# Gate scores on 32-column strips of the PE array, and one transpose to turn a group's scores back

## The chip, the cores and the metric

The kernel runs on one core of one Trainium2 chip, as one launch. The metric is the device time of that launch in microseconds (us). Three timed runs of the kernel before gave 1331.63, 1332.4 and 1335.52 us; the median is 1332.4 us.

## The reference, cut to what matters

Four blocks are applied in turn to 3125 rows of 256 features, each on the layer-normalised rows and added to the rows: a graph convolution of two layers (GNN 0), a mixture of 8 experts (FFN 0), a second graph convolution (GNN 1), a shared MLP with 4 small experts (FFN 1). The second layer of each graph convolution and the gate scores of the block that follows it are what the change is about:

```python
def _sage_conv(x, src, dst, Wl, bl, Wr):          # one layer
    agg = segment_sum(x[src], dst)                # sum over the neighbours
    mean = agg / max(cnt, 1)
    return mean @ Wl.T + bl + x @ Wr.T

x = x + _L0_gnn_ref(_layernorm(x), ...)           # two such layers
# FFN 0: x normalised, all in f32
gate_scores = x @ Wg + bg                         # 256 features to E = 8 scores a row
_, idx = top_k(gate_scores, 2)                    # the two best experts of each row
...
x = x + _L1_gnn_ref(_layernorm(x), ...)
# FFN 1
gates = softmax(x @ gW + gb)                      # 256 features to E = 4 scores a row
topv, topi = top_k(gates, 2)
```

## The kernel before, in words

The 3125 rows are padded to 25 tiles of 128. `adj` holds the matrix of edge counts in SBUF as f16, and a sum over neighbours is a product of `adj` with the rows, of which `l_parts` holds a high and a low f16 half. The function `second_conv` does the second layer of a graph convolution and, on the same rows, the norm and the gate scores of the block that follows. It is called twice: once with names that begin with `l_` (8 scores, `routing=True`, followed by the experts of FFN 0 in the same program block) and once with names that begin with `l1b_` (4 scores, followed by FFN 1). They are called the first and the second pass here.

In each pass TensorE (PE) first works through 25 steps of `dense` (f32, L2025) and `early` (tiles 0 to 9, L2049). Then it does one tile of rows after another, tiles 10 to 24 (`one_tile`): 50 matmuls of 128x256 f16 each (L2064). The rest is done for 7 groups of tiles of 4, 4, 4, 4, 4, 3 and 2 tiles (`SIZES`), and PE's part of it is put between the matmuls of `one_tile` by the table `BETWEEN`: the entry `(13, 1): [("rank", 0), ("score", 1)]` says that rank of group 0 and score of group 1 stand behind tile 13, and `(22, 0)` would be in the middle of tile 22. Per group:

- `turn(c)`: 2 transposes a tile, so that the features lie on the partitions (L2075, `l_dense`).
- ScalarE (ACT) takes them to SBUF, into `own` (L1975).
- `score(c)`: two matmuls, one for each half of the 256 features, with the gate's weights `wg` as the stationary operand (128 rows, 8 or 4 columns) and all the group's rows as the moving one (up to 512 columns), f32, into 8 or 4 partitions of the bank `extra` (L2084). The trace shows each f32 matmul as two passes with a weight load each.
- ACT copies that to `flat`, 8 or 4 partitions by up to 512 (L1986, `take_flat`).
- `back(c)`: one transpose a tile, of 8x128, to 128x8 in `l_sum` (L2095). For group 0 it waits until VectorE (DVE) has added the first ten tiles' sums, since it writes to the bank of the last two of them.
- DVE adds the bias. In the first pass it picks the two best experts (`choose`), PE sums the masks (`rank`, L2103 and L2104), DVE works out the places (`put`), and GpSimd (POOL) scatters the rows (L1757).

The order on each engine is the order in which the code issues; nothing reorders it. On the last tile, `BETWEEN[(24, 1)]` runs the rest of groups 5 and 6 one after another. In the second pass PE does products of FFN 1 there (`head`, L1488).

Before the groups, DVE sets up small things behind `take(24)`: L1907 to L1915.

Of the kernel before, what the change touches and what calls it, by code (L numbers as in the profile page):

```python
# [18 lines left out]
P = 128  # L19
D = 256  # L20
KD = D // P
# [1517 lines left out]
MOST = max(SIZES)  # L1539
assert STARTS[-1] == TILES  # L1540
# [35 lines left out]
def second_conv(nc, io, g, adj, parts, tag, names, gate, rows_from, rows_to, work, sums_left, routing=False, final=None):  # L1576
# [4 lines left out]
    with ExitStack() as ctx:  # L1581
# [26 lines left out]
        if routing:  # L1608
# [15 lines left out]
        wg = pr.sb("gate_w", [P, KD, E], F32)  # L1624
        bg = pr.sb("gate_b", [P, E], F32)
# [6 lines left out]
        flat = room[0:E, KD * MOST * P:(KD + 1) * MOST * P]  # L1632
# [4 lines left out]
        score_at, ranks_at, totals_at = (last_bank[:, at:at + MOST * E].rearrange("p (t e) -> p t e", e=E) for at in (0, 64, 128))  # L1637
# [4 lines left out]
            "ranked", "placed", "place_ready", "head_mm", "head_took", "init", "chain", "route_chain", "hi_in", "hi_used")  # L1642
# [141 lines left out]
        def _(dve):  # L1784
# [125 lines left out]
            dve.wait_ge(s["gate_in"], 32)  # L1910
            if routing:
                dve.wait_ge(s["consts"], 4)
                nc.vector.tensor_copy(row_id[:, :], row_i[:, :]).then_inc(s["init"], 1)
                nc.vector.memset(pre[:, MOST, :], 0.0).then_inc(s["init"], 1)
                nc.vector.tensor_copy(down[:, :], down_i[:, :]).then_inc(s["init"], 1)  # L1915
                dve.wait_ge(s["init"], 4)
                finish_early()
                for c in range(FINISHES):
                    choose(c)
                    put(c)  # L1920
                    if c + 2 < FINISHES:
                        finish(c + 2)
                nc.vector.tensor_copy(g["counts"][:, :], pre[:, SIZES[-1], :]).then_inc(s["init"], 1)
                dve.wait_ge(s["init"], 5)
                table.vector(dve)
                follow["vector"](dve)
            else:
                dve.wait_ge(s["init"], 1)
                finish_early()
                final.constants(nc, ch)  # L1930
                for c in range(FINISHES):
                    take_scores(c)
                    if c + 2 < FINISHES:
                        finish(c + 2)

        @block.scalar
        def _(act):
# [44 lines left out]
            def take_flat(c):  # L1982
                act.wait_ge(s["multiplied"], c + 1)
                if c >= 1:
                    act.wait_ge(s["scored"], c)
                nc.scalar.activation(flat[:, 0:SIZES[c] * P], extra[0:E, 0:SIZES[c] * P], ACT.Copy).then_inc(s["flat_ready"], 1)  # L1986
# [30 lines left out]
        def _(pe):  # L2017
# [61 lines left out]
            def score(c):  # L2079
                pe.wait_ge(s["xt_ready"], KD * (c + 1))  # L2080
                if c >= 1:
                    pe.wait_ge(s["flat_ready"], c)
                for f in range(KD):
                    ins = nc.tensor.matmul(extra[0:E, 0:SIZES[c] * P], wg[:, f, :], own[:, f, 0:SIZES[c] * P],  # L2084
                                           start=f == 0, stop=f == KD - 1)
                ins.then_inc(s["multiplied"], 1)

            def back(c):
# [5 lines left out]
                for t in range(SIZES[c]):  # L2094
                    ins = nc.tensor.transpose(score_at[:, t, :], flat[:, t * P:(t + 1) * P], g["ident"][0:E, 0:E])  # L2095
                ins.then_inc(s["scored"], 1)

            def rank(c):
# [4 lines left out]
                nc.tensor.matmul(last_bank[:, 64:64 + SIZES[c] * E], tri[:, :], mask[:, 0:SIZES[c], :], start=True, stop=True)  # L2103
                nc.tensor.matmul(last_bank[:, 128:128 + SIZES[c] * E], all1[:, :], mask[:, 0:SIZES[c], :], start=True, stop=True  # L2104
# [27 lines left out]
            pe.wait_ge(s["gate_in"], 32)  # L2132
# [799 lines left out]
```

## Time and profile before

| what | value |
|---|---|
| timed runs, median | 1332.4 us |
| profiled execution, span from first to last instruction | 1304.2 us |
| median less span, outside what the trace shows | 28.2 us |
| PE busy | 1220.4 us, 94% |
| DVE busy | 588.7 us, 45% |
| ACT busy | 360.1 us, 28% |
| POOL busy | 159.5 us, 12% |
| mean granted clock of PE | 0.980 |

PE is busy nearly all the time. Its matmuls are pipelined: a matmul's time in the trace is that from its start to its result, 273 ns for a 128x256 f16 one, while the next one starts long before that. What a group of matmuls costs PE is therefore read from the starts: from its first to the first of what follows. The first pass's tiles 10 to 24 lie at about 404 to 504 us of the span, the second's at about 1050 to 1154 us.

### The profile page before, as it was taken

What the parts mean: (1) busy time and instruction counts of PE and PEld (TensorE: products, weight loads), DVE (VectorE), ACT (ScalarE), POOL (GpSimd) and SP (SyncE); (2) the same over time, 40 slices, a digit from 0 to 9 for tenths busy, and PEclk for the clock granted to TensorE, in tenths of its full rate; (3) what the DMA queues carried; (4) which work ended last, traced back from release to release, by engine and by line L of the source; (5) the groups of instructions that cost most, each with busy time, mean ns of one, the idle gap of its engine ahead of it and who ended that gap; (6) DMA issues with size and microseconds to landing.
All of it is one profiled execution on the core that took longest, in us unless ns stands there. A gap on an engine that the chain in (4) does not pass through costs nothing. (4 is left out here: it accounts for less than half of the span.)

```text
span 1304.2 us, 22005 instructions
## 1 busy us (share of the span) xinstructions
PE 1220.4 (94%) x7906; PEld 913.8 (70%) x7906; DVE 588.7 (45%) x1563; ACT 360.1 (28%) x765; POOL 159.5 (12%) x151
## 2 busy tenths in 40 slices
PE   5969999998999997999999779999989999999998
PEld 3648888885667785787888657555556677866675
DVE  7968888853445657211111165000034363246544
ACT  3544444432221101333333234200022201124333
POOL 4100000000000336433443300000000000000000
PEclk9989999999999998999999979999999999999999
DMA  6400000014652235445655331120056434126001
GB/s 198 159 24 10 18 9 18 18 36 143 174 147 95 88 105 179 93 92 111 137 105 102 52 125 61 57 65 29 15 152 178 130 117 146 50 72 203 20 20 38
DMA packets 133085, 117.08 MB, mean 90 GB/s; under 512 B 22706, under 2 KB 121395, under 8 KB 133008
## 3 DMA queue, kind: packets, MB, share of 16 engines
q1 hardware_dynamic: 101760, 76.03, 20.1%
q0 software_dynamic: 11984, 18.77, 7.4%
q10 hardware_dynamic: 19264, 21.24, 4.8%
q8 instruction: 50, 0.82, 0.3%
q14 instruction: 27, 0.22, 0.1%
HBM read 67.01 MB, written 48.99 MB: 89 GB/s over the span
## 5 line engine op out<-in xcount | busy, mean ns | idle before, releaser
L1276 PE MATMUL b_pa<-adj,l_parts 128*128 (+1 forms) x1100 | 148.5, 287 | 2.5 <-ACT ring L1212 2.5
L1276 PEld LDWEIGHTS b_pa<-adj,l_parts 128*128 128x128 f16 x1100 | 104.9, 98 | 28.1 <-issue 4.4
L1218 ACT ACTIVATE adj<-b_pw 128x450 f32 (+1 forms) x176 | 86.8, 546 | 107.8 <-PE b_pw L1263 102.0
L561 DVE TENSOR_TENSOR ring<-it,key 128x1800 f16<-128x1800 f16 x88 | 96.4, 1096 | 36.3 <-PE b_pw L1263 36.0
L2400 PE MATMUL l_sum<-l_parts,ring 128*128 128x256 f32 x448 | 104.1, 385 | 5.2 <-ACT ring L2470 2.3
L2535 POOL DMA_INDIRECT x<-ring,l_ids_now x56 | 87.3, 1559 | 131.6 <-DVE ring L2500 103.2
L2400 PEld LDWEIGHTS l_sum<-l_parts,ring 128*128 128x128 f32 x448 | 82.9, 190 | 22.4 <-ACT ring L2470 12.3
L1263 PE MATMUL b_pw<-ring,room 128*128 128x150 f16 x1056 | 87.3, 233 | 9.9 <-DVE room L561 8.1
L2500 DVE TENSOR_TENSOR ring<-l_sum,l_parts 128x256 f32 (+1 forms) x56 | 23.6, 425 | 153.2 <-PE l_sum L2400 153.2
L1263 PEld LDWEIGHTS b_pw<-ring,room 128*128 128x128 f16 x1056 | 77.7, 100 | 15.2 <-DVE room L561 9.6
L2064 PE MATMUL l1b_sum<-l_parts,adj 128*128 128x256 f16 x750 | 86.5, 276 | 0.0
L2064 PE MATMUL l_sum<-l_parts,adj 128*128 128x256 f16 x750 | 84.9, 273 | 0.0
L561 DVE TENSOR_TENSOR room<-ib,low 128x1536 f16<-128x1536 f16 x88 | 83.8, 952 | 0.0
L2064 PEld LDWEIGHTS l1b_sum<-l_parts,adj 128*128 128x128 f16 x750 | 73.3, 99 | 13.5 <-issue 4.3
L2064 PEld LDWEIGHTS l_sum<-l_parts,adj 128*128 128x128 f16 x750 | 72.3, 98 | 12.9 <-issue 4.5
L1795 DVE SCALAR_TENSOR_TENSOR l_parts<-l1b_dense,scale,l_parts 128x256 f16<-128x256 f32 x25 | 12.1, 484 | 141.0 <-ACT l_parts L1950 141.0
L2755 ACT ACTIVATE l_parts<-m_bank,adj 128x320 f32<-128x320 f32 x82 | 42.7, 527 | 73.3 <-PE m_bank L2693 44.7
L2049 PEld LDWEIGHTS l_sum<-l_parts,adj 128*128 128x128 f16 x500 | 48.8, 98 | 19.9 <-issue 12.9
L2049 PEld LDWEIGHTS l1b_sum<-l_parts,adj 128*128 128x128 f16 x500 | 48.8, 98 | 19.4 <-issue 13.1
L501 PE MATMUL n_agg<-adj,l_parts 128*128 128x448 f16 (+1 forms) x300 | 60.6, 361 | 0.0
L2049 PE MATMUL l_sum<-l_parts,adj 128*128 128x256 f16 x500 | 58.5, 273 | 0.8 <-DVE l_parts L1795 0.8
L2049 PE MATMUL l1b_sum<-l_parts,adj 128*128 128x256 f16 x500 | 58.5, 273 | 0.4 <-DVE l_parts L1795 0.4
(384 smaller groups left out, 1741.4 us busy)
## 6 DMA issues: line engine op xcount, KB each, us to landing
ring<-sums_and_zt SPq DMA_DIRECT2D x50, 256.0 KB, 3.1
l_parts<-in_L_ffn_W SPq DMA_DIRECT2D x16, 512.0 KB, 5.0
l_parts<-slots_in SPq DMA_DIRECT2D x28, 257.0 KB, 2.7
pre<-room ACTq DMA_DIRECT2D x34, 128.0 KB, 1.8
ring<-inv SPq DMA_DIRECT2D x50, 64.0 KB, 3.7
sums_and_zt<-room ACTq DMA_DIRECT2D x5, 640.0 KB, 3.4
adj<-xt SPq DMA_DIRECT2D x5, 640.0 KB, 4.4
adj<-x SPq DMA_DIRECT2D x5, 640.0 KB, 5.7
```

Of the source, the lines that this page charges most:

```text
L501: ins = nc.tensor.matmul(pairs[n % 3][f][:, 0:size], parts[:, k, a, f * P:(f + 1) * P], moving, start=start and a == 0, stop=stop and a == 1)
L561: return nc.vector.tensor_tensor(out.rearrange("p r (h two) -> p r h two", two=2), names[:, 0:width].rearrange("p (h two) -> p h two", two ...
L1218: ins = nc.scalar.activation(adj[:, :, ds(group * GW * W + b * BANKW * W, BANKW * W)].rearrange("p k (w j) -> p w k j", j=W), pw[u % SLOT ...
L1263: ins = nc.tensor.matmul(to, low[:, n, :], sel[:, n, :], start=i == 0, stop=i == VIS - 1)
L1276: ins = nc.tensor.matmul(pa[f][:, :], parts[:, k, a, f * P:(f + 1) * P], adj[:, k, ds(r * BW, BW)], start=k == 0 and a == 0, stop=k == TIL ...
L1795: nc.vector.scalar_tensor_tensor(parts[:, k, 1, :], dense_bank[k % 2][:, 0:D], scale, parts[:, k, 0, :], ALU.mult, ALU.subtract).then_inc( ...
L2049: ins = nc.tensor.matmul(acc(t), adj[:, k, t * P:(t + 1) * P], parts[:, k, a, :], start=k == 0 and a == 0 and opens(t), stop=k == TILES - ...
L2064: ins = nc.tensor.matmul(acc(t), adj[:, k, t * P:(t + 1) * P], parts[:, k, a, :], start=k == 0 and a == 0 and opens(t), stop=k == TILES - ...
L2400: ins = nc.tensor.matmul(to[t], h[:, n, t * P:(t + 1) * P], w2[:, u, n, :], start=n == 0, stop=n == HB - 1)
L2500: nc.vector.tensor_tensor(y[:, half, t, :].rearrange("p a d -> p (a d)"), products[t], b2[:, u, :], ALU.add).then_inc(s["y_done"], 1)
L2535: pool.indirect_dma_start(out=g["x1"], in_=y[:, half, t, :], in_offset=None, compute_op=ALU.add, out_offset=bass.IndirectOffsetOnAxis(ap=i ...
L2755: nc.scalar.activation(to, b[:, 0:SUB], ACT.Relu, bias=bias).then_inc(s["act_took"], 1)
```

## The change

The gate's weights are copied once, by DVE, into `strips_of_wg`: 32 columns for each half of the features, of which the first 8 or 4 are the gate's and the rest are zero. `score` multiplies each row tile of 128 rows on its own: tile t of the group writes to partitions 32t to 32t+31 of `extra`, that is, through columns 32t to 32t+31 of the array. So it has 8 matmuls of 32x128 where it had 2 of 8x512. ACT copies 128 partitions by 128 (`flat`), and `back` is one transpose of 128x128. The scores then stand 32 columns apart in the bank, and the places of ranks and totals in it move to columns 128 and 192.

```diff
+STRIP = 32
+RANKS_AT, TOTALS_AT = MOST * STRIP, MOST * STRIP + 64
...
+        strips_of_wg = held[1][:, 0:KD * STRIP].rearrange("p (k e) -> p k e", k=KD)
...
-        flat = room[0:E, KD * MOST * P:(KD + 1) * MOST * P]
+        flat = room[:, KD * MOST * P:KD * MOST * P + P]
...
+            dve.wait_ge(s["pre_out1"], 16 * uses(1))
+            nc.vector.memset(strips_of_wg[:, :, E:STRIP], 0.0)
+            nc.vector.tensor_copy(strips_of_wg[:, :, 0:E], wg[:, :, :]).then_inc(s["gate_padded"], 1)
...
-                nc.scalar.activation(flat[:, 0:SIZES[c] * P], extra[0:E, 0:SIZES[c] * P], ACT.Copy).then_inc(s["flat_ready"], 1)
+                strips = SIZES[c] * STRIP
+                nc.scalar.activation(flat[0:strips, :], extra[0:strips, 0:P], ACT.Copy).then_inc(s["flat_ready"], 1)
...
+                if c == 0:
+                    pe.wait_ge(s["gate_padded"], 1)
...
                 for f in range(KD):
-                    ins = nc.tensor.matmul(extra[0:E, 0:SIZES[c] * P], wg[:, f, :], own[:, f, 0:SIZES[c] * P],
-                                           start=f == 0, stop=f == KD - 1)
+                    for t in range(SIZES[c]):
+                        ins = nc.tensor.matmul(extra[t * STRIP:(t + 1) * STRIP, 0:P], strips_of_wg[:, f, :], own[:, f, t * P:(t + 1) * P],
+                                               start=f == 0, stop=f == KD - 1)
...
-                for t in range(SIZES[c]):
-                    ins = nc.tensor.transpose(score_at[:, t, :], flat[:, t * P:(t + 1) * P], g["ident"][0:E, 0:E])
-                ins.then_inc(s["scored"], 1)
+                nc.tensor.transpose(last_bank[:, 0:P], flat[:, :], g["ident"][:, :]).then_inc(s["scored"], 1)
```

PE in the first pass, tile 12, from `score` of group 0 to behind its `back`, before (the sums are L2064, score L2084, back L2095):

```order
L2064 MATMUL l_sum<-l_parts,adj 128x256 x22
L2084 MATMUL l_extra<-room,l_gate_w 8x512 x2
L2064 MATMUL l_sum<-l_parts,adj 128x256 x26
L2095 MATMUL l_sum<-ident,room 128x8 x4
L2064 MATMUL l_sum<-l_parts,adj 128x256 x2
```

The same place of the changed kernel (the sums are L2073, score L2096, back L2106):

```order
L2073 MATMUL l_sum<-l_parts,adj 128x256 x22
L2096 MATMUL l_extra<-room 32x128 x8
L2073 MATMUL l_sum<-l_parts,adj 128x256 x26
L2106 MATMUL l_sum<-ident,room 128x128
L2073 MATMUL l_sum<-l_parts,adj 128x256 x2
```

Nothing is placed elsewhere among the sums; two matmuls became eight, and four transposes one.

DVE in the first pass, between the last step of `dense` and the sums of group 0, before (`l_tmp` is scratch of the norm; L1804 adds the bias to group 0's rows, L1810 its sums):

```order
L1907 TENSOR_SCALAR l_by_row<-l_by_row,unscale 128x25
L1908 MEMSET l_tmp 128x30
L1913 CAST l_row_id<-l_row_i 128x25
L1914 MEMSET l_pre 128x8
L1915 CAST l_down<-l_down_i 128x8
L1804 TENSOR_TENSOR l_rows<-l_rows,l_bias 128x4x256
L1810 SCALAR_TENSOR_TENSOR l_rows<-l_sum,l_by_row,l_rows 128x256 x4
```

The same place of the changed kernel:

```order
L1912 TENSOR_SCALAR l_by_row<-l_by_row,unscale 128x25
L1913 MEMSET l_tmp 128x30
L1917 MEMSET room 128x2x24
L1918 COPY room<-l_gate_w 128x2x8
L1921 CAST l_row_id<-l_row_i 128x25
L1922 MEMSET l_pre 128x8
L1923 CAST l_down<-l_down_i 128x8
L1809 TENSOR_TENSOR l_rows<-l_rows,l_bias 128x4x256
L1815 SCALAR_TENSOR_TENSOR l_rows<-l_sum,l_by_row,l_rows 128x256 x4
```

A memset and a copy now stand ahead of the sums of group 0.

## Rows read from the trace of the kernel before

**Rows 1.** Stretches of both passes; busy us (instructions) by engine, granted clock, DMA
```profile
425.00:500.00 75.00, 75.00 (x641) 61.48 (x641) 47.22 (x214) 7.51 (x16) 30.41 (x32) 1.00 0.30 101
1080.00:1150.00 70.00, 70.00 (x590) 56.22 (x588) 23.04 (x82) 6.21 (x14) 0.00 (x0) 1.00 0.30 97
```

**Rows 2.** Timeline of weight loads: start us, us, engine, line, what, [idle before]
```profile
1081.25 0.09 PEld L2084 LDWEIGHTS l1b_extra<-room,l1b_gate_w 128*4 128x4 f32 x2 [0.21 <-issue]
1081.68 0.09 PEld L2084 LDWEIGHTS l1b_extra<-room,l1b_gate_w 128*4 128x4 f32 x1 [0.34 <-issue]
1082.11 0.09 PEld L2084 LDWEIGHTS l1b_extra<-room,l1b_gate_w 128*4 128x4 f32 x1 [0.34 <-issue]
1083.06 0.22 PEld L2064 LDWEIGHTS l1b_sum<-l_parts,adj 128*128 128x128 f16 x3 [0.86 <-issue]
```

**Rows 3.** Timeline of PE, second pass, a turn and the sums behind it
```profile
1077.44 1.04 PE L2075 MATMUL l1b_dense<-ident,ring 128*128 128x128 f32 x8
1078.32 3.00 PE L2064 MATMUL l1b_sum<-l_parts,adj 128*128 128x256 f16 x26
```

**Rows 4.** Timeline of PE around back of group 1, second pass
```profile
1085.80 2.89 PE L2064 MATMUL l1b_sum<-l_parts,adj 128*128 128x256 f16 x25
1088.62 0.41 PE L2095 MATMUL l1b_sum<-ident,room 4*128 4x4 f32 x4
1088.96 2.25 PE L2064 MATMUL l1b_sum<-l_parts,adj 128*128 128x256 f16 x19
```

**Rows 5.** Timeline of PE, the two short matmuls of rank
```profile
431.39 0.18 PE L2103 MATMUL l_sum<-l_mask,l_tri 128*128 128x32 f16 x1
431.42 0.18 PE L2104 MATMUL l_sum<-l_mask,l_all 128*128 128x32 f16 x1
```

**Rows 6.** Line L2084, weight loads: ns min/median/max, first and last start us, forms
```profile
L2084 PEld LDWEIGHTS l_extra<-room,l_gate_w x28: 85/90/137, 418.6 to 512.0; 128*8 128x8 f32 x28
```

**Rows 7.** Timeline of PE, back of group 0 in either pass
```profile
424.74 0.38 PE L2095 MATMUL l_sum<-ident,room 8*128 8x8 f32 x4 [1.27 <-DVE ring L1810]
...
1072.84 0.38 PE L2095 MATMUL l1b_sum<-ident,room 4*128 4x4 f32 x4 [3.08 <-DVE ring L1810]
```

**Rows 8.** Timeline of DVE and PE at the start of tile 10, first pass
```profile
401.56 0.16 DVE L1915 CAST l_down<-l_down_i 128x8 f32<-128x8 int32 x1
401.57 0.07 DVE L1914 MEMSET l_pre<- 128x8 f32 x1
...
403.01 1.66 DVE L1810 SCALAR_TENSOR_TENSOR l_rows<-l_sum,l_by_row,l_rows 128x256 f32<-128x256 f32 x4
...
404.04 1.13 PE L2064 MATMUL l_sum<-l_parts,adj 128*128 128x256 f16 x8
```

**Rows 9.** Timeline of ACT's queue, store of tile 22; the page's line on such stores
```profile
395.94 0.33 ACTq L1945 DMA_DIRECT2D pre<-room  x1
...
pre<-room ACTq DMA_DIRECT2D x34, 128.0 KB, 1.8
```

**Rows 10.** Line L1986, ACT's copy of the scores
```profile
L1986 ACT ACTIVATE room<-l_extra x7: 373/586/586, 420.6 to 513.1; 8x512 f32<-8x512 f32 x5, 8x384 f32<-8x384 f32 x1, 8x256 f32<-8x256 f32 x1
```

**Rows 11.** Timeline, end of the first pass
```profile
511.17 1.88 PE L2084 MATMUL l_extra<-room,l_gate_w 128*8 128x256 f32 x4 [0.75 <-ACT room L1975]
...
512.21 0.18 DVE L1873 TENSOR_TENSOR l_mask<-l_one 128x24 f16<-128x24 f32 x1
...
512.98 0.20 PE L2103 MATMUL l_sum<-l_mask,l_tri 128*128 128x24 f16 x1
```

**Rows 12.** Timeline of PE, scores of groups 5 and 6, second pass
```profile
1154.01 1.45 PE L2084 MATMUL l1b_extra<-room,l1b_gate_w 128*4 128x384 f32 x4
...
1163.03 1.03 PE L2084 MATMUL l1b_extra<-room,l1b_gate_w 128*4 128x256 f32 x4
```

**Rows 13.** Stretches around back of group 0, second pass; columns as in rows 1
```profile
1069.00:1073.00 4.00, 0.92 (x10) 0.62 (x9) 3.70 (x11) 0.00 (x0) 0.00 (x0) 1.00 0.00 0
1073.00:1077.00 4.00, 4.00 (x26) 3.00 (x26) 3.44 (x17) 0.00 (x0) 0.00 (x0) 0.60 0.01 4
```

More of the change, by code:

```diff
@@ L1539 @@
 MOST = max(SIZES)
+STRIP = 32
+RANKS_AT, TOTALS_AT = MOST * STRIP, MOST * STRIP + 64
+assert MOST * STRIP == P
 assert STARTS[-1] == TILES
@@ L1636, in second_conv @@
         last_bank = sum_bank[LATE_BANKS]
-        score_at, ranks_at, totals_at = (last_bank[:, at:at + MOST * E].rearrange("p (t e) -> p t e", e=E) for at in (0, 64, 128))
+        score_at = last_bank[:, 0:MOST * STRIP].rearrange("p (t e) -> p t e", e=STRIP)[:, :, 0:E]
+        ranks_at, totals_at = (last_bank[:, at:at + MOST * E].rearrange("p (t e) -> p t e", e=E) for at in (RANKS_AT, TOTALS_AT))
         s = {n: pr.sem(n) for n in (
@@ L1641, in second_conv @@
             "norm_done", "turned", "xt_ready", "xt_out", "multiplied", "flat_ready", "scored", "score_done", "consts", "pool_chain", "mask_ready",
-            "ranked", "placed", "place_ready", "head_mm", "head_took", "init", "chain", "route_chain", "hi_in", "hi_used")
+            "ranked", "placed", "place_ready", "gate_padded", "head_mm", "head_took", "init", "chain", "route_chain", "hi_in", "hi_used")
             + tuple(f"x_in{u}" for u in range(XB)) + tuple(f"pre_out{u}" for u in range(XB)) + tuple(f"in{r}" for r in range(RING)) + tuple(f"rows_in{c}" for c in range(FINISHES))
@@ L2102, in rank @@
                 pe.wait_ge(s["mask_ready"], c + 1)
-                nc.tensor.matmul(last_bank[:, 64:64 + SIZES[c] * E], tri[:, :], mask[:, 0:SIZES[c], :], start=True, stop=True)
-                nc.tensor.matmul(last_bank[:, 128:128 + SIZES[c] * E], all1[:, :], mask[:, 0:SIZES[c], :], start=True, stop=True
+                nc.tensor.matmul(last_bank[:, RANKS_AT:RANKS_AT + SIZES[c] * E], tri[:, :], mask[:, 0:SIZES[c], :], start=True, stop=True)
+                nc.tensor.matmul(last_bank[:, TOTALS_AT:TOTALS_AT + SIZES[c] * E], all1[:, :], mask[:, 0:SIZES[c], :], start=True, stop=True
                                  ).then_inc(s["ranked"], 1)
@@ L2131, in _ @@
                     dense(k + 2)
-            pe.wait_ge(s["gate_in"], 32)
             pe.wait_ge(s["z_done"], TILES)
```

## The prediction

> **What bounds the kernel here.** I read the stretches first. From 425 to 500 us (first pass) and from 1080 to 1150 us (second pass) PE is busy for 75.00 of 75 and 70.00 of 70 us at a granted clock of 1.00, while DVE has 47.22 and 23.04 us of work and ACT under 8 [rows 1]. So there a matmul that goes shortens the kernel by what it occupies on PE. Then I read the timeline around each kind of piece that stands between the sums, to get its price from the starts, and last the two ends of a pass, where PE waits for others.
>
> The unit: a run of 26 sums takes 3.00 us; less the 0.27 us of the last one, over 25 steps, that is 0.109 us for each [rows 3]. A turn of 8 f32 transposes of 128x128 takes from 1077.44 to 1078.32, 0.11 us each, with nothing lost at either end [rows 3].
>
> Score of a full group: the weight loads stand at 1081.25, 1081.68 and 1082.11, so a pass of 512 columns takes 0.43 us, and there are four (two loads merged in the first row). The next sum starts at 1083.06, and not at 1081.25 + 4 x 0.43 = 1082.97 [rows 2]: 0.09 us are lost on leaving. On entering as much: the 26 sums before should be over at 1078.32 + 2.83 = 1081.15 [rows 3], and the score starts at 1081.25 [rows 2]. So a score costs 1.72 + 0.18 = 1.90 us.
>
> Back of a full group: 25 sums from 1085.80 should end at 1088.53; the sums go on at 1088.96, so four small transposes cost 0.43 us [rows 4].
>
> **The change part by part.**
>
> Back. One 128x128 f32 transpose is of the same form as those of a turn, so 0.11 us [rows 3] in place of 0.43 [rows 4]: 0.32 us less. Groups 1 to 4 of both passes stand among the sums, 8 x 0.32 = 2.6 us. This part is the surest.
>
> Score. Eight matmuls of 128 columns are 16 passes of 0.43 / 4 = 0.107 us each, 1.72 us if they are done one after another, as before. What the change can win is that two strips stream at the same time. No row of the trace shows two matmuls on different columns of the array, so I bound it. Upper end of the cost: none beside another, 1.90 us with both ends, no gain. Lower end: only the issue of matmuls bounds it. The shortest distance between two matmuls in the trace is 0.03 us (431.39 to 431.42, [rows 5]); 15 such steps, a last stream of 0.11 and both ends of 0.18 are 0.74 us, a gain of 1.16. I take a case between. The passes are issued in the order strip 0 first and second pass, strip 1 first and second pass, and so on. Two passes on the same columns follow one another at the full stream (0.43 apart for 512 columns, [rows 2]), so the second pass of a strip starts 0.107 after the first, but the next strip's first pass may start right behind the start of that one. A pair then takes 0.107 to 0.137 us, with the step of [rows 5] as the upper figure: 7 pairs and a last one of 0.214 are 0.96 to 1.17, with 0.18 at the ends 1.14 to 1.35. That is a gain of 0.55 to 0.76; I take 0.65. For groups 1 to 4 of both passes: 8 x 0.65 = 5.2 us.
>
> The Trainium skill, "TensorE: Matmul & The Clock Gate", part on packing small matmuls, says that matmuls on different column strips run at the same time and start about 4 ns apart. With 0.004 in place of 0.03 the step of a pair is 0.111, the gain is 0.73, and the 5.2 us would be 5.8 (an estimate from that page); no row here can show it. The same part says that a weight load lies beside a running matmul only where the row groups differ; here all strips use all 128 rows. Its result is the third rival below. Against it speaks [rows 2], where two loads on all 128 rows stand within one row at the start of a stream.
>
> Group 0. Its back waits for DVE's sums, 1.27 us in the first pass and 3.08 in the second [rows 7]. PE gets there earlier by what score 0 saves and waits longer by as much, so score 0 counts nothing. Its back still has to run after the wait; it gets shorter by about 0.1 in each pass (four short transposes take 0.31 us to the next sum, one takes about 0.2): 0.2 us.
>
> DVE's new work ahead of group 0: a memset of 0.07 and a small copy of 0.16 us, [rows 8] for instructions of that size, about 0.2 us as they overlap. In the first pass tile 10 waits for the second of the four L1810, which ends at 403.01 + 0.39 + 0.48 = 403.88, and starts at 404.04 [rows 8]: no slack, and the later back of group 0 hangs on the same chain of DVE. So +0.2 us. In the second pass the chain has a few tenths of slack there: I take +0.1. The wait for the store of tile 22 costs nothing: it is issued at 395.94 [rows 9], over 5 us before DVE comes to it at about 401.5, and such stores take 1.8 us from issue to landing [rows 9]. If it did bind, all of group 0 would be late by the overrun.
>
> ACT's copy drops from 586 ns [rows 10] by perhaps 0.3 us for a quarter of the columns. Among the sums nothing waits for it, as half a tile of sums, 2.7 us, stands between score and back. I count 0.
>
> End of the first pass. DVE sets the pace there, not PE: rank of group 5 needs the mask that DVE has at 512.21 + 0.18 = 512.39, and starts at 512.98, since score of group 6 stands ahead of it on PE from 511.17 [rows 11]. Its four passes of 256 columns take twice their usual time there, at half clock (1.88 us against 1.03 in [rows 12]). With strips it is over by the time of the mask, so up to 0.55 us come off DVE's chain; I take 0.5. The score of group 5 there lies beside DVE's work: 0.
>
> End of the second pass. PE's pieces are in a row with ACT's. Score of group 5 (three tiles) gains 3/4 of 0.65 = 0.5. Score of group 6 would gain 0.3, but PE waits for ACT around it: 0.2. The two backs: 0.2. Together 0.9 us.
>
> Sum: 2.6 + 5.2 + 0.2 - 0.3 + 0.5 + 0.9 = 9.1 us less. The profiled execution would go from a span of 1304.2 to 1295.1. The 28.2 us between span and median stay, so 1332.4 - 9.1 = 1323.3 us.
>
> **The rivals.**
>
> 1. Full overlap: all four strips stream together. The gain of a score is 1.16: 8 x 0.51 more, and 0.6 more at the end of the second pass, 4.7 us on top: 1318.6. For it: nothing in the trace forbids it. Against it: the order of issue, two passes on one strip in a row.
>
> 2. No overlap: strips stream one after another. The scores gain nothing. There remain 2.6 + 0.2 + 0.2 (backs at the end) - 0.3 = 2.7 us: 1329.7. For it: every two long f32 matmuls in this trace follow at the full stream, whatever their width in columns of the array (4 columns in [rows 2]).
>
> 3. Slower: the weights of a strip are not loaded while another strip streams. The price of a load is 0.09 us [rows 6], and there are 16 in a full score where 4 were hidden. That is 16 x 0.09 = 1.44 us more for each of 8 scores, 11.5; 1.8 for the 20 passes of groups 5 and 6 at the end of the second pass, 0.7 for score 6 ahead of rank in the first, 0.2 for score 0, where 1.44 outgrows the wait of 1.27. 14.2 less the 2.7 of rival 2 are 11.5 us more: 1343.9. It decides from about 0.02 us a pass on, where 8 x 16 x 0.02 eats the 2.7.
>
> 4. The clock. In the second pass PE idles 3.08 us before back 0, and in 1073 to 1077 us the granted clock is 0.60, while it was 1.00 in the 4 us before [rows 13]: about 1.6 us are lost. With the change the first pass's wait grows from 1.27 to about 2.1 us. If the clock falls there as well, 1.6 us come back: 1324.9. It goes with any of the cases above.
>
> **How the numbers follow.** Forecast (pairs overlap, with or without rival 4, which I give 1 in 6 within it) 0.50; full overlap 0.11; no overlap 0.23; slower 0.16. The least change that a measurement of this kernel can tell is about 0.3%, 4.0 us. The first two are faster by more than that, no overlap is within it, the third rival is slower by more. So faster 0.61, same 0.23, slower 0.16. The range: low end 1317, a little below full overlap; high end 1336, which takes in no overlap with a late DVE and the milder half of exposed loads. Some 0.15 lies above and little below.
>
> **What would show it.** In the changed kernel's timeline: score at about 1.2 us of PE against 1.81, with starts of alternating distance 0.107 and under 0.03; back at 0.11. Starts 0.107 apart throughout mean rival 2, 0.19 rival 3, and 0.03 rival 1. Waits of back 0 of about 2.1 and 3.8 us show score 0 swallowed. Rank of group 5 right behind its mask shows the end of the first pass. The prediction is wrong if PE, now sooner, meets a wait among the sums of tiles 13 to 24 (for a mask, a norm or places); DVE's 47.22 of 75 us makes that unlikely.

## The result, and the profile after

| what | before | after |
|---|---|---|
| timed runs, median (lowest to highest) | 1332.02 (1329.08 to 1335.52) us | 1317.74 (1315.36 to 1321.14) us |
| ratio | | 0.9878, interval 0.9851 to 0.9906 |
| forecast | | 1323.3 us, range 1317 to 1336 |

The change makes the kernel faster, by about 1.2%, 14.3 us between the medians. The forecast was 9.1 us. The ratio on the 1332.4 us that the forecast started from is 1316.1 us, just below its range; the interval of the ratio reaches from 1312.5 to 1319.9 us.

First, how the numbers stand to one another. The runs came in sets, each on one chip, and the kernel before takes about 1306 us in two sets (chips 4 and 1) and about 1330 us in two others (chip 0, and the set of the result, whose chip the record doesn't name). They are called quick and slow chips here. Each named chip served in one set only, so it isn't shown that the chip makes the difference and not the hour. By its span of 1304.2 us, the trace in front of the prediction is of the quick kind; the timed runs of 1332 us are of the slow kind. So times are compared within one set, and traces only between sets of one kind. The trace of the changed kernel that came with the result is from a slow chip; its page says:

```profile
span 1318.5 us, 22227 instructions
PE 1215.4 (92%) x8014; PEld 918.8 (70%) x8014; DVE 588.9 (45%) x1567; ACT 356.1 (27%) x765; POOL 159.4 (12%) x151
L2073 PE MATMUL l_sum<-l_parts,adj 128*128 128x256 f16 x750 | 93.6, 284 | 12.2 <-issue 11.9
L2073 PE MATMUL l1b_sum<-l_parts,adj 128*128 128x256 f16 x750 | 87.1, 277 | 0.0
```

The sums of the first pass have 12.2 us of idle time before them, those of the second none. This idle time goes with the slow chip (last section); it is there in the kernel before as well.

What answers to [rows 1 to 4] is read from a trace of the changed kernel on a quick chip (`after_again`, span 1290.2 us). Stretches of both passes, columns as in [rows 1]:

```profile
425.00:492.00 67.00, 67.00 (x662) 59.80 (x661) 43.72 (x198) 6.28 (x16) 29.48 (x31) 1.00 0.33 110
1080.00:1137.00 57.00, 57.00 (x554) 50.46 (x553) 21.40 (x75) 4.71 (x12) 0.00 (x0) 1.00 0.29 91
```

PE is still busy throughout at the full granted clock. Timeline of PE in the second pass, from turn of group 1 to behind its back:

```profile
1071.28 1.04 PE L2084 MATMUL l1b_dense<-ident,ring 128*128 128x128 f32 x8
1072.15 3.00 PE L2073 MATMUL l1b_sum<-l_parts,adj 128*128 128x256 f16 x26
1075.09 0.64 PE L2096 MATMUL l1b_extra<-room 128*32 128x128 f32 x16
1075.66 5.63 PE L2073 MATMUL l1b_sum<-l_parts,adj 128*128 128x256 f16 x50
1081.13 0.27 PE L2106 MATMUL l1b_sum<-ident,room 128*128 128x128 f32 x1
1081.24 0.93 PE L2073 MATMUL l1b_sum<-l_parts,adj 128*128 128x256 f16 x7
```

From these starts, as in the prediction: the 26 sums should be over at 1072.15 + 26 x 0.109 = 1074.98. The score starts 0.11 later and the next sum 0.57 after that, so a score costs 1075.66 - 1074.98 = 0.68 us, where it was 1.90 [rows 2]. Over the whole list a full score costs 0.67 us. The back costs 1081.24 - 1081.13 = 0.11 us, where it was 0.43 [rows 4].

The same score, cut off after 4, 8 and 12 passes by stretches that end earlier, shows how the 16 lie:

```profile
1075.09 0.32 PE L2096 MATMUL l1b_extra<-room 128*32 128x128 f32 x4
1075.09 0.43 PE L2096 MATMUL l1b_extra<-room 128*32 128x128 f32 x8
1075.09 0.54 PE L2096 MATMUL l1b_extra<-room 128*32 128x128 f32 x12
```

A single pass lasts 0.27 to 0.30 us from start to result. Four of them are over after 0.32 us, and each further four add 0.11, up to the 0.64 of all 16: the passes go in four waves of four, one per strip, and a wave takes the 0.107 us of one stream. The first four starts are 20 ns from the first to the last, about 7 ns apart. This is full overlap, the first rival.

Scores of groups 5 and 6, second pass, answer to [rows 12]:

```profile
1141.56 0.64 PE L2096 MATMUL l1b_extra<-room 128*32 128x128 f32 x12
1142.13 2.42 PE L1488 MATMUL l1b_sum<-adj 128*128 128x320 f32 x8
...
1149.77 0.63 PE L2096 MATMUL l1b_extra<-room 128*32 128x128 f32 x8
1150.33 1.34 PE L1488 MATMUL l1b_sum<-adj 128*128 128x320 f32 x4
```

They take PE 0.57 and 0.56 us to the next product; two or three strips take as long as four. ACT's copy of a group's scores, 586 ns in [rows 10], is 277:

```profile
L1995 ACT ACTIVATE room<-l_extra x7: 271/277/278, 419.2 to 505.4; 128x128 f32<-128x128 f32 x5, 96x128 f32<-96x128 f32 x1, 64x128 f32<-64x128 f32 x1
```

### The profile page after: what moved, and what is told of

It is laid out like the page before. It is cut to its first block and busy times, and to the rows that moved or that the text cites. A ratio compares the mean times of both kernels' runs of the same rounds, so it can differ in the third digit from the quotient of the medians.

```text
span 1318.5 us, 22227 instructions
## 1 busy us (share of the span) xinstructions
PE 1215.4 (92%) x8014; PEld 918.8 (70%) x8014; DVE 588.9 (45%) x1567; ACT 356.1 (27%) x765; POOL 159.4 (12%) x151
## 5 line engine op out<-in xcount | busy, mean ns | idle before, releaser
L2073 PE MATMUL l_sum<-l_parts,adj 128*128 128x256 f16 x750 | 93.6, 284 | 12.2 <-issue 11.9
L2073 PEld LDWEIGHTS l_sum<-l_parts,adj 128*128 128x128 f16 x750 | 75.1, 102 | 28.3 <-issue 17.7
L2073 PE MATMUL l1b_sum<-l_parts,adj 128*128 128x256 f16 x750 | 87.1, 277 | 0.0
L2073 PEld LDWEIGHTS l1b_sum<-l_parts,adj 128*128 128x128 f16 x750 | 74.1, 99 | 10.6 <-issue 1.2
L2058 PEld LDWEIGHTS l_sum<-l_parts,adj 128*128 128x128 f16 x500 | 48.8, 98 | 20.6 <-issue 12.9
L2058 PE MATMUL l_sum<-l_parts,adj 128*128 128x256 f16 x500 | 58.5, 273 | 1.6 <-DVE l_parts L1800 1.6
```

The costliest lines, as they stand in the source:

```text
L2058: ins = nc.tensor.matmul(acc(t), adj[:, k, t * P:(t + 1) * P], parts[:, k, a, :], start=k == 0 and a == 0 and opens(t), stop=k == TILES - ...
L2073: ins = nc.tensor.matmul(acc(t), adj[:, k, t * P:(t + 1) * P], parts[:, k, a, :], start=k == 0 and a == 0 and opens(t), stop=k == TILES - ...
```

## The experiments

### The two kernels again, on a quick chip

`before_again` is the kernel before and `after_again` the changed kernel, both unchanged.

> The kernel before, unchanged, for a second trace. Its first trace has a span of 1304.2 us, while its timed runs have 1329 to 1336; the changed kernel's profiled run has 1.5 us between span (1318.5) and time (1320.04), not 28.2. Theory A (the first trace caught a rare quick execution): span near 1330, with pauses of PE among the sums of tiles 10 to 24 of the first pass (more than 10 us in all of starts over 0.3 us apart with no wait named), as in the changed kernel's trace at 444 to 516 us. Theory B (28 us always lie outside the span): span near 1304 again and no such pauses.

Measured: 1305.36 us, span 1303.9, granted clock 0.98. So the trace of 1304.2 us was the usual one of such a chip, and only 1.5 us lie outside the span, not 28.2.

> The changed kernel, unchanged. If the 14.3 us are the change's own: ratio 0.987 to 0.991. The pauses of PE among the sums of the first pass (about 4.5 us in each of four groups) are then in this trace too or not; if they come and go, the times of its runs spread by up to 15 us.

Measured: 1293.72 us (1290.92 to 1297.77) against 1306.32, ratio 0.9911, interval 0.9894 to 0.9927; span 1290.2. The two traces, place by place:

| stretch | before_again | after_again | difference |
|---|---|---|---|
| start to tile 10, first pass | 403.55 | 403.93 | +0.38 |
| tile 10 to behind back of group 0 | 21.05 | 19.57 | -1.49 |
| from there to the last sum | 79.23 | 73.89 | -5.35 |
| last sum to the first product of the experts' second layer | 21.82 | 22.12 | +0.30 |
| from there to tile 10 of the second pass | 524.43 | 525.00 | +0.57 |
| tile 10 to behind back of group 0 | 22.69 | 22.67 | -0.02 |
| from there to the last sum | 80.66 | 74.17 | -6.49 |
| last sum to the products behind the pass | 14.25 | 12.74 | -1.51 |
| the rest | 136.19 | 136.13 | -0.06 |
| sum | 1303.9 | 1290.2 | -13.7 |

Most of the gain lies between back of group 0 and the last sum, where PE is hardly ever idle. Four scores and four backs there give 4 x (1.24 + 0.33) = 6.3 us in each pass.

These 13.7 us are of one pair of traces, and a favourable one. The traced run of `after_again` took 1291.72 us, 2.0 less than the median of its set, and the medians differ by 12.6 us (12.9 in the other set on a quick chip). A second trace of the changed kernel, `after_third`, has a span of 1293.5, 10.4 less than `before_again`. The first pass makes most of this spread. From tile 10 to the last sum it takes 100.3 us in both quick traces of the kernel before; in the changed kernel it takes 93.5 (`after_again`), 96.3 (`after_third`) and 97.0 (`later_second`, further down, whose first pass is that of the changed kernel). The second pass takes 96.8 and 97.0, against 103.4.

### The back alone

```diff
-                nc.tensor.transpose(last_bank[:, 0:P], flat[:, :], g["ident"][:, :]).then_inc(s["scored"], 1)
+                for _ in range(4):
+                    ins = nc.tensor.transpose(last_bank[:, 0:P], flat[:, :], g["ident"][:, :])
+                ins.then_inc(s["scored"], 1)
```

> As the changed kernel, but back issues its one transpose four times over, 0.44 us in place of 0.11, about what four small ones took before (0.43). Theory: back is worth 0.32 us a group, 2.6 us among the sums and some 0.5 at the ends; so 3 us slower than the changed kernel, ratio to before near 0.991. Rival (the time hangs on pauses and not on PE's work): no difference.

Measured: 1297.18 us, ratio to before 0.9929, interval 0.9915 to 0.9942, against 0.9911 of the changed kernel on the same chip: 3.5 us slower. Timeline of PE, second pass:

```profile
1083.77 1.58 PE L2073 MATMUL l1b_sum<-l_parts,adj 128*128 128x256 f16 x13
1085.19 0.60 PE L2107 MATMUL l1b_sum<-ident,room 128*128 128x128 f32 x4
1085.62 0.60 PE L2073 MATMUL l1b_sum<-l_parts,adj 128*128 128x256 f16 x4
```

Four transposes cost 0.43 us, as before [rows 4], though these are 128x128 and those were 8x128 or 4x128. One costs 0.11. So the number of transposes sets the cost of the back, and not how many of the 128 rows hold data; 8 x 0.33 = 2.6 us of the gain are its. All these transposes load 128 columns of weights each (8x128, 4x128 or 128x128), and no run changes that, so whether the load or the instruction makes the 0.11 us is not shown. The intervals of the two ratios overlap (0.9915 to 0.9942 and 0.9894 to 0.9927), so it is the trace that gives the size.

### The same work on one strip

All tiles go through columns 0 to 31 of the array; the copy of 32x512 and four transposes of 32x128 follow from that. So this run takes back the gain of the score and that of the back together. The four passes of a tile also stand in a row in the order of issue here; the next run changes only that.

```diff
-                for f in range(KD):
-                    for t in range(SIZES[c]):
-                        ins = nc.tensor.matmul(extra[t * STRIP:(t + 1) * STRIP, 0:P], ...
+                for t in range(SIZES[c]):
+                    for f in range(KD):
+                        ins = nc.tensor.matmul(extra[0:STRIP, t * P:(t + 1) * P], ...
...
-                nc.scalar.activation(flat[0:strips, :], extra[0:strips, 0:P], ...
+                nc.scalar.activation(flat[:, 0:SIZES[c] * P], extra[0:STRIP, 0:SIZES[c] * P], ...
...
-                nc.tensor.transpose(last_bank[:, 0:P], flat[:, :], g["ident"][:, :]) ...
+                for t in range(SIZES[c]):
+                    ins = nc.tensor.transpose(last_bank[:, t * STRIP:(t + 1) * STRIP], flat[:, t * P:(t + 1) * P], g["ident"][0:STRIP, 0:STRIP])
```

> All strips on the same 32 columns: the same 8 f32 matmuls of 32x128, but each writes to partitions 0 to 31 of extra at its own columns, ACT copies 32x512 and back is four transposes of 32x128; per tile both halves of the features in turn. Theory (the gain is the overlap of different column strips): score back at 1.7 to 1.9 us on PE and a time within 3 us of the kernel before. Rival (small matmuls are cheap on any columns, the overlap of strips is not needed): score under 1.2 us.

Measured: 1307.06 us, ratio 1.0011, interval 1.0001 to 1.002; span 1305.6. With eight matmuls, the padded weights and DVE's two new instructions, but one strip and four transposes, the whole gain is gone. Timeline of PE and, in the last row, of its weight loads:

```profile
1082.19 1.93 PE L2095 MATMUL l1b_extra<-room,l1b_third 128*32 128x128 f32 x16
1084.06 5.63 PE L2072 MATMUL l1b_sum<-l_parts,adj 128*128 128x256 f16 x50
...
1082.19 1.67 PEld L2095 LDWEIGHTS l1b_extra<-room,l1b_third 128*32 128x32 f32 x16 [0.21 <-issue]
```

16 passes take 1.87 us to the next sum on one strip, and 0.57 on four; with what is lost on entering, a score costs 1.96 us here, 1.91 in the kernel before and 0.67 in the changed one. Its four transposes cost 0.46. The passes stand 0.11 apart here, so even 16 loads on one strip are hidden behind the streams.

### The order of issue

```diff
-                for f in range(KD):
-                    for t in range(SIZES[c]):
+                for t in range(SIZES[c]):
+                    for f in range(KD):
```

Now four passes on one strip follow each other before the next strip has any.

> As the changed kernel, but score takes the tiles in the outer loop and the two halves of the features in the inner one, so that the four passes of a strip (two matmuls, two passes each) stand one behind another in the order of issue. Theory A (PE starts passes strictly in the order of issue, so strips only overlap where neighbours in that order are on different columns): three of four steps are on the same strip, score at 1.5 to 1.8 us, time 4 to 8 us over the changed kernel. Theory B (each strip has its own order, a later strip does not wait for an earlier one): score still at 0.67 to 0.7 us and no difference.

Measured, on a slow chip: 1313.27 us against 1329.43, ratio 0.9888, interval 0.9858 to 0.9917; the change itself had 0.9878 on such a chip. Timeline of PE:

```profile
1094.82 1.47 PE L2073 MATMUL l1b_sum<-l_parts,adj 128*128 128x256 f16 x12
1096.22 0.67 PE L2096 MATMUL l1b_extra<-room 128*32 128x128 f32 x16
1096.82 1.38 PE L2073 MATMUL l1b_sum<-l_parts,adj 128*128 128x256 f16 x11
```

From the score to the next sum are 0.597 us, against 0.577 in the changed kernel (on the slow chip of the result as on quick ones): the order costs 0.02 us. The score cut off after its first four passes:

```profile
1096.22 0.34 PE L2096 MATMUL l1b_extra<-room 128*32 128x128 f32 x4
```

That is 0.02 more than in `after_again`. The starts of the first four passes are 13 to 14 ns apart now, where they were about 7. In both kernels this is 3.4 ns for each pass that the issue order puts on a strip before the next one begins (four here, two there), and two more passes ahead of each of three strips are the 0.02 us. The trace doesn't name the strip of a pass; but on one strip passes stand 0.109 us apart (`one_strip`), so four that start within 0.04 us are on four strips. So a pass that waits for its own strip does not hold back the passes issued behind it on other strips.

### Choosing before the norm at the end of the first pass

In the changed kernel PE waits 0.8 us for the mask of group 4 at the end of the first pass. Here DVE makes this mask before it norms group 5.

```diff
+                if routing and c == 5:
+                    choose(4)
...
-                    choose(c)
+                    if c != 4:
+                        choose(c)
```

> As the changed kernel, but in the first pass DVE does choose of group 4 ahead of the wait for the store of group 5's rows and of their norm, not behind. Theory (the new wait of 1.0 us of PE for the mask of group 4 delays its places, and with them the scatters that the experts wait for): rank of group 4 runs without a wait, the first product of the experts starts about 1 us sooner after tile 24's beginning; time 1 us less than the changed kernel, ratio to before 0.990. Rival (turn of group 5 becomes late by as much, or the start of the experts hangs on something else): no difference.

Measured, on a slow chip: 1315.83 us, ratio 0.9899, interval 0.9873 to 0.9925. This says nothing: on that chip PE pauses among the sums, and the mask is in time anyway. It was run again on a quick chip.

> Choose of group 4 ahead of the wait for group 5's store, for a trace beside the changed kernel's on the same chip. In the last run PE paused so much in the first pass that the mask would have been in time anyway. On a chip without pauses: no wait at rank 4 (1.0 us in the changed kernel), and from the last sum of the first pass to the first product of the experts no more than the 22.1 us there.

Measured: 1297.32 us, a single run, beside 1295.0 for the changed kernel on the same chip. Timeline of PE:

```profile
494.53 0.88 PE L2087 MATMUL l_dense<-ident,ring 128*128 128x128 f32 x6 [0.82 <-DVE ring L1833]
495.24 0.18 PE L2116 MATMUL l_sum<-l_mask,l_tri 128*128 128x32 f16 x1
```

Rank of group 4 no longer waits, but the turn of group 5 ahead of it now waits 0.82 us for the norm. The same time of DVE stands in front of one or the other. From the last sum to the first product of the experts' second layer it takes 23.8 us, where 22.1 or less was expected and `after_third` has 22.2. My theory, that the 0.8 us could be had back by DVE's order, falls.

### Backs and ranks placed later

PE waits longest at back of group 0. Here it stands one tile later. Turn, score and back of groups 1 and 2, back of group 3 and the ranks of groups 0 to 2 move by half a tile or a tile; the scatters of groups 0 to 2 follow their ranks.

```diff
-BETWEEN = {(11, 1): [("turn", 0)], (12, 0): [("score", 0)], (12, 1): [("back", 0)],
-           (13, 0): [("turn", 1)], (13, 1): [("rank", 0), ("score", 1)], (14, 1): [("back", 1)],
-           (15, 1): [("turn", 2)], (16, 0): [("rank", 1), ("score", 2)], (17, 0): [("back", 2)],
-           (18, 1): [("turn", 3)], (19, 0): [("rank", 2), ("score", 3)], (20, 0): [("back", 3)],
+BETWEEN = {(11, 1): [("turn", 0)], (12, 0): [("score", 0)], (13, 1): [("back", 0), ("turn", 1)],
+           (14, 0): [("score", 1)], (14, 1): [("rank", 0)], (15, 1): [("back", 1)],
+           (16, 1): [("turn", 2), ("rank", 1)], (17, 0): [("score", 2)], (18, 0): [("back", 2)],
+           (18, 1): [("turn", 3)], (19, 0): [("score", 3)], (19, 1): [("rank", 2)], (20, 1): [("back", 3)],
```

> As the changed kernel, but back of group 0 stands behind tile 13, not tile 12, and turn, score, rank and back of groups 1 and 2 (and rank 2, back 3) move later by half a tile to a tile. Theory (back 0's waits of 1.5 and 4.8 us for DVE's sums, and the half clock after the second, are lost for no reason but the place): both waits go, no half clock near them; 5 to 7 us less than the changed kernel, ratio to before 0.985 to 0.987. Rival (DVE's chain is late in any case and the wait turns up at turn 2 or rank 1 instead): no difference, and a new wait of 2 us or more there.

Measured, on a slow chip: 1308.12 us against 1329.43, ratio 0.9834, interval 0.9803 to 0.9865. The change alone had 0.9878 on a slow chip, with an interval that overlaps this one, and `tile_outer`, which differs from it by little, 1313.27 us on the same chip. The comparison was repeated on a quick chip, beside the changed kernel (`after_third`) and a kernel that has the later places in the second pass alone (`later_second`).

> Later places in both passes, again, beside the one with them in the second pass alone. In the first pass they take away the wait before back 0 (1.5 us) but bring new ones (1.3 us at back 2, 2.8 at turn 4 in the last run): equal to later places in the second pass alone, or up to 3 us slower.

> The changed kernel again, beside the next kernels on the same chip. On a chip where the kernel before takes near 1306 us: 1293 to 1295. Where it takes near 1330 us (pauses of PE of some 15 to 18 us in the first pass in both kernels): 1314 to 1318.

> The changed kernel with the later places of back 0 and of groups 1 and 2 in the second pass alone; the first pass keeps its places. Theory (of the 7.2 us between the changed kernel and the one with later places in both passes, all are in the second pass: 4.8 of wait before back 0 and 2.4 of half clock): 7 us less than the changed kernel on the same chip, ratio to before near 0.984 to 0.986, and no wait of PE before back 0 in the second pass. Rival (the second pass's wait hides something that the end then waits for): 2 us less or nothing.

Measured, before at 1307.86 us:

| kernel | median us | ratio | interval | span |
|---|---|---|---|---|
| after_third | 1295.0 | 0.9902 | 0.9887 to 0.9916 | 1293.5 |
| later_second | 1291.05 | 0.9866 | 0.9848 to 0.9883 | 1290.5 |
| later_backs_again | 1289.92 | 0.987 | 0.9852 to 0.9889 | 1287.5 |

Both beat the kernel before by 17 to 18 us, and the change by 4 to 5 us. The interval of `later_second` lies wholly below that of `after_third`; that of `later_backs_again` meets it at its edge. What they remove is seen in the changed kernel (`after_again`), around back of group 0 in the second pass: the timeline of PE, then two stretches.

```profile
1066.94 0.44 PE L2106 MATMUL l1b_sum<-ident,room 128*128 128x128 f32 x1 [4.28 <-DVE ring L1815]
```

```profile
1063.00:1067.00 4.00, 0.06 (x1) 0.09 (x2) 3.59 (x10) 0.00 (x0) 0.00 (x0) 0.97 0.00 0
1067.00:1071.00 4.00, 4.00 (x23) 2.93 (x24) 3.55 (x18) 0.00 (x0) 0.00 (x0) 0.60 0.00 0
```

PE idles 4.28 us for DVE, and then works 4 us at a granted clock of 0.60, mostly at the lower level, 1.2 GHz. `later_second` at its back of group 0, timeline of PE, and the stretch behind it:

```profile
1069.74 4.20 PE L2073 MATMUL l1b_sum<-l_parts,adj 128*128 128x256 f16 x37
1073.78 0.27 PE L2106 MATMUL l1b_sum<-ident,room 128*128 128x128 f32 x1
1073.89 1.04 PE L2084 MATMUL l1b_dense<-ident,ring 128*128 128x128 f32 x8
```

```profile
1074.00:1078.00 4.00, 4.00 (x49) 3.38 (x47) 2.90 (x13) 1.08 (x2) 0.00 (x0) 1.00 0.36 110
```

No wait and a clock of 1.00: the stretch from tile 10 to the last sum goes from 96.95 us (`after_third`) to 91.3, 5.6 less, where 7 were expected. 4.3 of them are the wait; the other 1.3 come from the lower clock. The medians differ by 4.0 us. In the first pass the later places bring waits of their own (rank of group 1 waits 1.62 us for its mask, say), and what they give there is not told apart by these intervals (1291.05 and 1289.92 us).

### The kernel before, on a slow chip

> The kernel before, unchanged, once more. If this chip is one on which it takes near 1332 us, its trace should show pauses of PE among the sums of the first pass, as the changed kernel's first trace does; if it takes near 1306 us, none.

Measured: 1328.16 us, span 1326.3. The waits of PE in the first pass (436 to 522 us), of this kernel and then of the changed one that came with the result; columns: what waited, for what, us in all, times, longest:

```profile
PE l_sum L2064 <- issue: 8.9, 16, 1.1
```

```profile
PE l_sum L2073 <- issue: 11.9, 16, 1.1
```

On a quick chip PE has no such wait among its sums in either kernel.

## Why the prediction was wrong, point by point

**The step that failed** is the term of the scores. The prediction put it so: "Two passes on the same columns follow one another at the full stream ..., so the second pass of a strip starts 0.107 after the first, but the next strip's first pass may start right behind the start of that one." It took the array to be one queue, in which the second pass of strip 0 holds back strip 1. The runs show otherwise: 16 passes start in waves of four, and `tile_outer`, where the queue would be held up longest, costs 0.02 us more and not several times 0.107. The score costs 0.67 us and not 1.25, so its gain was 1.24 us, not 0.65: 8 x 0.59 = 4.7 us. `one_strip` shows that the other strips are its whole cause, since without them 16 passes cost what they did before (1.96 and 1.91 us).

The Trainium skill, "TensorE: Matmul & The Clock Gate", Part 3, on packing small matmuls, says that matmuls on different column strips run together, with starts about 4 ns apart. The prediction quoted it, and used it only to shorten a pair. The trace agrees with the overlap. Its starts are about 7 ns apart, but each f32 matmul is two passes; for a pass it is 3.4 ns, in `tile_outer` too.

With 1.24 in its place, and 0.6 more at the end of the second pass, the forecast would have been 14.4 us, 1318.0 of 1332.4 us or 0.9892, near the first rival's 1318.6. Measured were 0.9911 and 0.9902 on quick chips, and 0.9878 on the slow one. The intervals of 0.9902 and 0.9878 hold it; that of 0.9911 begins just above. That rival had 0.11 of the chance, on the ground of the order of issue. The weight on it was wrong by this one assumption, which no row of the trace before could support or refute.

**The lower bound of the score** was too high as well: 15 steps of the shortest distance in the trace, 0.03 us [rows 5], gave 0.74 us, and the cost is 0.67, with starts 7 ns apart within a wave. That distance was of two matmuls on all 128 columns; it is no bound for matmuls on different columns.

**Back** was right: 0.33 us each for a forecast of 0.32, and in `four_backs` a back costs 0.43 again.

**Exposed loads**, the third rival, did not come. The record of weight loads of one score (`after_again`):

```profile
1075.09 0.38 PEld L2096 LDWEIGHTS l1b_extra<-room 128*32 128x32 f32 x16 [0.21 <-issue]
```

16 loads begin and end within 0.38 us while the passes run. A load takes 0.11 us here (the price of 0.09 in [rows 6] was that of 8 columns), so 16 of them one after another would be 1.76 us, over twice what the score takes: they lie beside the passes and beside one another. The Trainium skill, on the same page and part, says in one sentence that a load overlaps a running matmul only where their row groups differ; another sentence there also lets a load go ahead into a background weight buffer. All strips here use all 128 rows, so by the first sentence the loads should have stood alone, and the measurement goes against it.

**Group 0** was right for the second pass: score 0 saved 1.21 us up to the back, and wait and back together grew by 1.19. The wait went from 3.08 [rows 7] to 4.28 us, forecast 3.8, short by the mis-sized score. In the first pass it went from 1.27 only to 1.26, and 1.49 us were gained: DVE had the sums of group 0 earlier there. That is not stable: in `after_third` the same wait is 2.56 us and in `later_second` 3.04, and the stretch takes 20.98 and 21.46 us, as in the kernel before or more. Why DVE's sums come up to 1.8 us earlier or later is open.

**The clock**, the fourth rival, was seen in those two runs. Two stretches of `after_third`, first pass:

```profile
421.00:425.00 4.00, 1.53 (x14) 1.12 (x12) 3.57 (x8) 0.00 (x0) 0.00 (x0) 1.00 0.00 0
425.00:429.00 4.00, 3.91 (x21) 2.87 (x22) 2.48 (x13) 0.00 (x0) 0.00 (x0) 0.57 0.00 0
```

After 2.56 us of idle PE, its granted clock is 0.57 for 4 us, where `after_again` has 1.00 behind a wait of 1.26. The sums behind it take 75.36 us to the last one, against 73.89. In `later_second` the clock is 0.62 from 426.4 to 430.4 us, behind the wait of 3.04, and they take 75.51. So the mechanism was right, and it took its microsecond and a half in two of the three traces from quick chips with this first pass. The prediction gave it 1 in 6.

**DVE's new instructions** were forecast at 0.2 us for the first pass; tile 10 starts 0.38 us later in `after_again`. The two traces of the changed kernel on quick chips differ by as much there (403.93 and 404.36), and so do those of the kernel before (404.04 and 403.55), so a term of this size can't be told.

**The end of the first pass** was wrong in its sign. Rank of group 5 does stand close behind its mask now, as forecast, and score 6 takes 1.07 us in place of 1.88:

```profile
504.27 1.07 PE L2096 MATMUL l_extra<-room 128*32 128x128 f32 x8 [0.75 <-ACT room L1983]
...
505.31 0.18 DVE L1878 TENSOR_TENSOR l_mask<-l_one 128x24 f16<-128x24 f32 x1
505.55 0.20 PE L2113 MATMUL l_sum<-l_mask,l_tri 128*128 128x24 f16 x1 [0.21 <-DVE l_mask L1878]
```

But nothing came of it. The stretch from the last sum to the first product of the experts' second layer took 0.30 us more, where 0.5 less was forecast; it is 22.12 and 22.21 us in the changed kernel, and 22.15 and 21.82 in the kernel before. The experts begin when the rows of group 4 are scattered (ACT waits for `scattered4`), and that hangs on rank 4, not rank 5:

```profile
494.34 0.19 DVE L1878 TENSOR_TENSOR l_mask<-l_one 128x32 f16<-128x32 f32 x1
494.59 0.19 PE L2113 MATMUL l_sum<-l_mask,l_tri 128*128 128x32 f16 x1 [0.80 <-DVE l_mask L1878]
497.65 0.96 POOL L1762 DMA_INDIRECT slots_in<-ring,place  x1 [3.55 <-DVE place L1899]
...
512.57 0.60 ACT L2474 ACTIVATE l_parts<-l_dense 128x512 f32<-128x512 f32 x1 [6.91 <-DMA slots_in<-ring,place]
```

From the first scatter of group 4 to ACT are 14.9 us here, and 14.5 in `before_again` (504.10 to 518.60). The prediction took the wait that ended last on PE for the one that decides. The same rows show the new wait that it called unlikely: PE is now ahead of DVE and waits 0.80 us for the mask of group 4, though DVE is busy only 43.72 of 67 us. It takes about 1 us of the first pass's 6.3.

**The end of the second pass** gave 1.51 us for a forecast of 0.9. Most of the term is the gains of scores 5 and 6, which were mis-sized as the others were.

**The 28.2 us** "between span and median" were no part of the run, but for 1.5 of them. The rest was the difference of two sets of runs. The forecast kept them as a constant, so they did no harm to the sum; only the rule that what is outside the trace stays had no ground.

In the sum: 9.1 us forecast, 4.7 more for eight scores, 0.6 more for the end of the second pass, 1.4 more from group 0 in the first pass; less 1.0 for the new wait for a mask, 0.8 for the end of the first pass, 0.2 for DVE, and 0.6 by which the work between the passes is longer in this trace, which the runs don't explain. That is 13.2, and 13.7 were measured between the two spans. The terms of the first pass and of the work between the passes are of this one pair: with `after_third` the two spans differ by 10.4 us, mostly because the 1.4 from group 0 are gone and the clock takes 1.5. The same work between the passes takes 523.8 to 527.1 us in the traces from quick chips, so 0.6 there means nothing. On a slow chip the gain of 14.3 us can't be laid out like this: there is one trace of either kernel, and the pauses in them differ.

## What to carry to other kernels

A matmul that uses few columns of the array can be cut along its moving rows into four, each on a strip of 32 columns, and the four then stream in the time of one, in both orders of issue that were tried; this paid 1.24 us for each score of 512 rows with 4 or 8 results a row. A transpose cost 0.11 us whether it turned 4, 8 or 128 partitions of 128 columns, so put the pieces on different partitions and turn all of them with one. Once PE has less to do, look again at each place where it meets another engine: another 4 to 5 us came from moving small operations on PE by about a tile, since a long wait cost its own length and then 1.3 to 1.5 us more through the lower clock.

## What the runs showed of the hardware

**Strips have an order of their own.** Passes on one strip follow 0.109 us apart (`one_strip`), while passes on the other three start beside them. In `tile_outer` passes on later strips start ahead of passes that were issued before them, so the description's sentence that nothing reorders the work of an engine holds on PE only within a strip. Each pass issued ahead of the next strip's first one delays it by 3.4 ns. On entering and leaving such a score about 0.1 us are still lost each, as before [rows 2].

**Sets of runs differ by 1.8%.** The kernel before takes 1306.32 and 1307.86 us in the two sets of runs on quick chips, and 1329.43 and 1332.02 in those on slow ones. Most of the difference is in the first pass: from tile 10 to the last sum it takes 116.9 us (`before_third`) against 100.3 (`before_again`). Timeline of POOL and PE in the changed kernel on a slow chip:

```profile
463.24 0.96 POOL L1762 DMA_INDIRECT slots_in<-ring,place  x1 [0.30 <-issue]
464.51 0.96 POOL L1762 DMA_INDIRECT slots_in<-ring,place  x1 [0.30 <-issue]
465.50 0.27 PE L2073 MATMUL l_sum<-l_parts,adj 128*128 128x256 f16 x1 [1.05 <-issue]
465.77 0.96 POOL L1762 DMA_INDIRECT slots_in<-ring,place  x1 [0.30 <-issue]
466.91 0.38 PE L2073 MATMUL l_sum<-l_parts,adj 128*128 128x256 f16 x2 [1.14 <-issue]
```

PE stops for about 1 us at a time between sums, waiting for nothing that the profile shows, while POOL issues its indirect scatters; and its granted clock falls, to 0.93 as the mean from 425 to 500 us. The pauses come in bursts, in both kernels, and in none of the traces from quick chips, though the scatters run there too. What causes them stays open. A kernel without the scatters, which would tell, was not tried, and no chip was used in two sets.
